# A neighbourhood attention layer rewritten as a preparation stage and an attention stage, with gathered surroundings and scores made twice

## The reference, cut to what matters

```python
x = x + _L0_conv_ref(_gn(x), ...)          # relative positions
x = x + _L1_conv_ref(_gn(x), registers, qkv_w, qkv_b, out_w, out_b)
x = x + _L2_conv_ref(_gn(x), ...)          # relative positions
x = x + _L3_conv_ref(_gn(x), ...)          # rotary, with a mask
# _L1_conv_ref, 12 heads of 16 channels, a window of 7x7 tokens clipped to the image:
qkv = x @ qkv_w.T + qkv_b
reg_kv = registers @ qkv_w[D_MODEL:].T + qkv_b[D_MODEL:]
k_cat, v_cat = concatenate([k, reg_k]), concatenate([v, reg_v])
scores = einsum('bnqe,bnke->bnqk', q, k_cat) / sqrt(16)
scores = where(mask_cat, scores, -1e30)     # 49 neighbours and the 16 registers
o = einsum('bnqk,bnke->bnqe', softmax(scores), v_cat)
return o @ out_w.T + out_b
```

## Time and profile before

| | |
|---|---|
| median of 3 runs | 9050.09 us (9038.95 to 9065.04) |
| the profiled execution | 9057.34 us, of which 9055.6 us are the span of the trace |
| TensorE, VectorE, ScalarE, GpSimd busy | 81%, 58%, 48%, 25% of the span |
| the window layer's two blocks | 2360.21 to 3985.64 us of the span |

### The profile page before, as it was taken

How to read it: one execution, slowest core, us unless ns; L and a number is a source line. 1 busy time by engine, 2 the same in 40 slices (tenths; PEclk the granted TensorE clock), 3 DMA queues, 4 the chain that set the end, 5 groups by cost and what they waited for, 6 DMA issues and landing times. The chain is left out here.

```text
span 9055.6 us, 188790 instructions
## 1 busy us (share of the span) xinstructions
PE 7343.7 (81%) x62744; PEld 4481.5 (49%) x62744; DVE 5241.4 (58%) x8043; ACT 4335.9 (48%) x8449; POOL 2240.3 (25%) x2715
## 2 busy tenths in 40 slices
PE   2999999989388777846998999899556499999998
PEld 2555555555155555534555555555222255555555
DVE  3655555556255555553555555555588666666665
ACT  1444444444265656541444444445111277777776
POOL 2343434343121211214343434332111000000000
PEclk7989999999698999976998999899777799999999
DMA  6757666766433334346767565764312254445443
GB/s 160 134 114 142 124 131 119 138 120 112 110 74 70 74 68 76 69 119 117 142 119 129 115 135 117 132 121 82 101 56 80 78 133 112 122 119 127 116 119 90
DMA packets 536711, 999.82 MB, mean 110 GB/s; under 512 B 102258, under 2 KB 303027, under 8 KB 500211
## 3 DMA queue, kind: packets, MB, share of 16 engines
q1 hardware_dynamic: 479346, 900.50, 45.7%
q0 software_dynamic: 56576, 88.90, 6.5%
HBM read 645.95 MB, written 335.81 MB: 108 GB/s over the span
## 5 line engine op out<-in xcount | busy, mean ns | idle before, releaser
L1676 DVE TENSOR_REDUCE a_nmp<-a_S 128x2 f32<-128x1024 f32 x1536 | 1878.2, 1224 | 1362.7 <-PE a_S L1524 1347.3
L1777 ACT ACTIVATE a_PROB<-a_T 128x512 f32<-128x512 f32 x3072 | 1667.6, 595 | 1959.9 <-PE a_T L1503 1949.0
L1373 POOL CAST a_RF<-a_RL 32x512 fp32r<-32x512 f32 x1536 | 1295.0, 843 | 1120.8 <-DVE a_RL L1704 1028.8
L2492 DVE CUSTOM_DVE_ANT_0 a_X<-a_S,a_mask 128x1024 f32<-128x1024 f32 x768 | 910.0, 1223 | 551.9 <-PE a_S L2388 548.5
L1499 PE MATMUL a_T<-a_QW,a_KW 64*128 64x512 f32 x3072 | 813.4, 522 | 300.4 <-issue 135.3
L2533 ACT ACTIVATE a_PROB<-a_T 128x512 f32<-128x512 f32 x1536 | 835.8, 601 | 382.9 <-PE a_T L2402 382.9
L1499 PEld LDWEIGHTS a_T<-a_QW,a_KW 64*128 64x128 f32 x3072 | 313.8, 193 | 1312.3 <-issue 1309.3
L1537 PE MATMUL a_O<-a_PROB,a_V 128*32 128x512 f32 x6144 | 929.5, 681 | 2.5 <-ACT a_PROB L1777 2.5
L2402 PE MATMUL a_T<-a_ident,a_X 128*128 128x128 f32 x6144 | 824.7, 277 | 101.8 <-DVE a_OSB L2509 98.1
L962 DVE CUSTOM_DVE_ANT_0 a_PROB<-a_S,a_mask 128x512 f32<-128x512 f32 x768 | 522.8, 688 | 591.9 <-PE a_PT L799 498.4
L2402 PEld LDWEIGHTS a_T<-a_ident,a_X 128*128 128x128 f32 x6144 | 671.8, 141 | 303.0 <-issue 285.3
(11 more groups left out here) (158 smaller groups left out, 9847.0 us busy)
## 6 DMA issues: line engine op xcount, KB each, us to landing
a_QV<-a_part_rows SPq DMA_DIRECT2D x384, 256.0 KB, 7.2
a_rel_rows<-a_RF SPq DMA_DIRECT2D x96, 1024.0 KB, 9.2
a_K<-part_rows SPq DMA_DIRECT2D x576, 128.0 KB, 4.0
a_X<-xn_scratch SPq DMA_DIRECT2D x72, 768.0 KB, 6.7
stream<-a_Y POOLq DMA_DIRECT2D x288, 192.0 KB, 4.6
a_part_rows<-a_part SPq DMA_DIRECT2D x48, 1024.0 KB, 12.2
a_QV<-a_part_rows SPq DMA_DIRECT2D x384, 128.0 KB, 7.8
a_QV<-a_rel_rows SPq DMA_DIRECT2D x384, 128.0 KB, 6.4
```

Source lines behind the costliest of these rows:

```text
L1373: nc.gpsimd.tensor_copy(dst, src).then_inc(permuted, 1)
L1676: nc.vector.tensor_reduce(nmp[:, qh, c, 2 * pr:2 * pr + 2, kh], S[:, pr], AX.X, ALU.max).then_inc(s_done, 1)
L1777: nc.scalar.activation(PROB[:, s % PRING, 2 * pr + sd], T[:, slot(("st", s, pr, sd))], ACT.Exp).then_inc(t_act, 1)
L2492: nc.vector.tensor_tensor_reduce(out=X[:, v % 2, c, g], in0=S[:, sd].rearrange("p a b -> p (a b)"), in1=mask[:, n % 2, g, c], scale=1.0, s ...
```

## The change

The window layer's blocks become `prepare_win` and `attend_win`; the other layers keep theirs.

`prepare_win` goes once over the images. It normalises an image, and GpSimd gathers for each quadrant of 16x16 queries the 19x19 tokens around it, with the 16 registers put between their lines: 377 keys, padded to 384. TensorE projects the queries (four pieces of 512), the keys of the four quadrants (eight pieces of 384) and the values (twelve chunks of 128 keys), all heads at once. VectorE and ScalarE split queries and keys in two F32R parts, and SP stores all three in DRAM.

`attend_win` has 24 units again, each now four quadrants ("turns") of 256 queries, and each turn three steps, one for each 128 of its 384 keys. An operand has 79 rows: 48 of split queries or keys, 16 and 13 that code the window's rows and columns (so the mask comes out of the matmul), and 2 that carry the row maximum. The scores are made twice. `straight` makes them queries by keys for the maximum alone, two turns ahead: four items a turn, each two heads, reduced by `row_max`. `combine` splits the maximum, `turn_max` transposes it, and `take_max` writes it into the two rows of the query operand. `transposed` then makes the scores keys by queries, maximum already subtracted; ScalarE exponentiates them from PSUM, and the result is the moving operand of `values` without a transpose or a copy. PSUM tiles for `transposed`, `turn_max` and the tail of the unit before share a ring of three. In a step TensorE issues the first pair of heads of `transposed`, then `values` of the step before, then `straight`, then the second pair.

```diff
-KEYS_W = 4 * P
+NEAR = 3 * P
+NEAR_CHUNKS = 12
...
+def prepare_win(nc, sems, name, x_in, stream_out, w, gavg, q_rows, k_rows, v_rows, near_lines):
+    RING, BLOCKS = 6, 3
+    QUADS = 4
+    ORDER = [("q", m, t) for m in range(2) for t in range(2)]
+    for j in range(6):
+        ORDER += [("k", *divmod(j, QUADS)), ("v", j, 0)]
+    ORDER += [("k", 1, 2), ("k", 1, 3)]
+    PIECES = [n for n in ORDER if n[0] != "v"]
...
+            def gather(b):
+                s = b % 2
+                pool.wait_ge(xn_ready, 2 * b + 2)
+                need(pool, t_ready, done(b - 2, ORDER[-1], "pe") if b > 1 else 0)
+                alone(pool)
+                for quad in range(QUADS):
+                    y, x, n = 13 * (quad // 2), 13 * (quad % 2), before_regs(quad)
+                    image = XN[:, s].rearrange("p k (y x) -> p k y x", x=SIDE)
+                    at = 19 * n
+                    nc.gpsimd.tensor_copy(XG[:, s, :, quad, 0:at].rearrange("p k (y x) -> p k y x", x=19),
+                                          image[:, :, y:y + n, x:x + 19]).then_inc(gathered, 1)
+                    nc.gpsimd.tensor_copy(XG[:, s, :, quad, at + REGS:19 * 19 + REGS].rearrange("p k (y x) -> p k y x", x=19),
...
+                if n[0] == "q":
+                    _, m, t = n
+                    image = XN[:, s].rearrange("p k (y x) -> p k y x", x=SIDE)
+                    for right in range(2):
+                        for k in range(2):
+                            last = nc.tensor.matmul(T[0:HALF, to, 256 * right:256 * right + 256],
+                                                    wq[:, k, m * HALF:(m + 1) * HALF],
+                                                    image[:, k, 16 * t:16 * t + 16, 16 * right:16 * right + 16],
+                                                    start=k == 0, stop=k == 1)
+                elif n[0] == "k":
+                    _, m, quad = n
+                    for k in range(2):
+                        last = nc.tensor.matmul(T[0:HALF, to, 0:NEAR], wk[:, k, m * HALF:(m + 1) * HALF], XG[:, s, k, quad],
+                                                start=k == 0, stop=k == 1)
+                else:
+                    for a in range(2):
+                        quad, c = divmod(2 * n[1] + a, NEAR // P)
+                        here = slice(CHANNELS * a, CHANNELS * a + CHANNELS)
+                        for k in range(2):
+                            nc.tensor.matmul(T[:, to, here], XG[:, s, k, quad, P * c:P * c + P], wv[:, k],
+                                             start=k == 0, stop=False)
+                        last = nc.tensor.matmul(T[:, to, here], one_line[:], bv_line[:], start=False, stop=True)
+                last.then_inc(t_ready, 1)
+
+            pe.wait_ge(consts_loaded, CONSTS)
+            pe.wait_ge(set_up, SETUP)
+            alone(pe)
+            mean(0)
...
+def attend_win(nc, sems, name, stream, w, ident, q_rows, k_rows, v_rows, near_lines):
+
+    UNITS = GROUPS * IMAGES
+    QUADS, CHUNKS_N = 4, NEAR // P
+    STEPS = QUADS * CHUNKS_N
+    RING, PRING, BUFS = 3, 3, 3
+    WIDE = 2 * P
+    ROWS = 3 * DIM + 16 + 2 + 13
+    TURNS_N = QUADS * UNITS
+    SPANS = {(0, 0): (0, 256, 0, 226), (0, 1): (94, 284, 0, 284), (1, 0): (0, 284, 0, 284), (1, 1): (128, 256, 24, 226)}
+    ITEMS = {0: (0, 1), 1: (2,), 2: (3,)}
+    TAIL = {2: "sum", 3: "turn0", 5: "turn1", 6: "wo00", 8: "wo01", 9: "wo10", 11: "wo11"}
+    NM_AT = 1
...
+                for sd in range(2):
+                    g = 2 * pr + sd
+                    last = nc.tensor.matmul(S[:, n % 2, sd, 0:width],
+                                            Q_[0:ROWS, s, g, WIDE * quad + P * tile:WIDE * quad + P * tile + P],
+                                            K[0:ROWS, s, g, NEAR * quad + at:NEAR * quad + at + width], start=True, stop=True)
+                last.then_inc(s_ready, 1)
...
+            def values(u, s):
+                quad, kc = divmod(s, CHUNKS_N)
+                t = QUADS * u + quad
+                pe.wait_ge(t_act, TALLY[("t", u, s, 1)])
+                if s == 0:
+                    pe.wait_ge(v_loaded[u % BUFS], 16 * (u // BUFS + 1))
+                if kc == 0:
+                    need(pe, o_out, t)
+                alone(pe)
+                for g in range(G):
+                    last = nc.tensor.matmul(O[Q * g:Q * g + Q, t % 2], V[:, u % BUFS, s, g], PROB[:, (STEPS * u + s) % PRING, g],
+                                            start=kc == 0, stop=kc == CHUNKS_N - 1)
+                last.then_inc(pv_done, 1)
+
...
+                    transposed(u, s, 0)
+                    if s:
+                        values(u, s - 1)
+                    elif u:
+                        values(u - 1, STEPS - 1)
+                    if t + 2 < TURNS_N:
+                        for i in ITEMS[kc]:
+                            straight(t + 2, i)
+                    transposed(u, s, 1)
+                    if kc == NM_AT and t + 1 < TURNS_N:
+                        turn_max(t + 1)
+                    if u and s in TAIL:
+                        tail(TAIL[s], u - 1)
...
+            def combine(t):
+                e = t % 2
+                eng.wait_ge(s_done, 4 * t + 4)
+                nc.vector.tensor_copy(nm_hi[:, e], nm[:, e]).then_inc(nm_ready, 1)
+                eng.wait_ge(nm_ready, t + 1)
+                nc.vector.tensor_copy(nm_wide[:, e, :, 0:P:Q], plain(nm_hi[:, e])).then_inc(nm_split, 1)
+                nc.vector.tensor_tensor(nm_wide[:, e, :, 1:P:Q], nm[:, e], plain(nm_hi[:, e]), ALU.subtract).then_inc(nm_split, 1)
...
-        normalise_block(nc, sems, f"n{i}", x, xn, streams[i], w["bo"], a["gavg"])
-        if kind == "rel":
...
+            prepare_win(nc, sems, f"n{i}", x, streams[i], w, a["gavg"], q_rows, k_rows, near_rows, near_lines)
+            attend_win(nc, sems, f"a{i}", streams[i], w, a["ident"], q_rows, k_rows, near_rows, near_lines)
...```

On TensorE, two tiles of a unit in `attend_block` before stood so (a_S scores, a_PT the transposed probabilities, a_O outputs):

```order
L799 MATMUL a_PT<-a_ident,a_PROB 128x128 x4
L782 MATMUL a_S<-a_KK,a_QQ 128x384
L782 MATMUL a_S<-a_KK,a_QQ 128x128
L799 MATMUL a_PT<-a_ident,a_PROB 128x128 x4
L814 MATMUL a_O<-a_PTS,a_V 16x128 x16
```

More of the change, by code:

```diff
@@ L317, in attend_block @@
[L317 to L329, removed]
@@ L431, in attend_block @@
-        jobs = []
-        def job(step, pe, dve=(), act=()):
-            jobs.append((step, pe, list(dve), list(act)))
-        def project(w_sb, rows, half):
-            def run(n, par):
-                cols = slice(STARTS[half], STARTS[half] + WIDTHS[half])
-                if rotary:
-                    cols = slice(0, BANK)
-                    if half == 1:
-                        nc.tensor.wait_ge(loaded_more, 16 * 3 * (n + 1))
-                        alone(nc.tensor)
-                for k in range(2):
-                    last = nc.tensor.matmul(M[0:rows, 0:cols.stop - cols.start], w_sb[:, k, :], X[:, k, cols],
-                                            start=k == 0, stop=k == 1)
-                return last
-            return run
@@ L469, in add_v_jobs @@
-        def add_v_jobs(step, halves):
-            for i, half in enumerate(halves):
-                job(step + 2 * i, project(wv_sb, G * DIM, half), act=[v_out(half)])
-                run, place = turn_v(half)
-                job(step + 2 * i + 1, run, act=[place])
-        def free_whole(n, piece):
-            before = UNIT_STEPS * n + SPLIT_STEPS * piece - (REL_STEPS if piece == 0 else 0)
-            need(nc.vector, split, before, solo=True)
-            if rel:
-                need(nc.vector, moved, 16 * G * (PIECES * n + piece), solo=True)
@@ L892, in epilogue, with free @@
-            def epilogue():
-                n = UNITS - 1
-                output(n, 1, CHUNKS - 1)
-                before = lambda: tail_out(pe, n, 0, 2)
-                for half, which in TAIL_AFTER.values():
-                    tail(n, half, which, before)
-                    before = lambda half=half, which=which: tail_out(pe, n, half, which)
-            pairs(pe, prologue, body, epilogue)
+            def free(b, n):
+                i, v = ORDER.index(n) - RING, b
+                if i < 0:
+                    i, v = i + len(ORDER), v - 1
+                if v >= 0:
+                    pe.wait_ge(out_of[kind(ORDER[i])], done(v, ORDER[i], kind(ORDER[i])))
@@ L1018, in _ @@
+            rest(NP * IMAGES - 1)
         @block.scalar
         def _(act):
[L1020 to L1034 removed]
@@ new lines, in values @@
+            def values(b, j):
+                s = b % 2
+                act.wait_ge(t_ready, done(b, ("v", j, 0), "pe"))
+                if j == 0:
+                    need(act, v_stored[s], 16 * (b // 2))
+                alone(act)
+                nc.scalar.copy(VT[:, s, 2 * j:2 * j + 2, :, 0:DIM],
+                               T[:, ORDER.index(("v", j, 0)) % RING, 0:2 * CHANNELS].rearrange(
```

(7 more changed lines are left out.)

1173 lines of the change are left out of this document (536 added, 637 removed).

## The result

| | median us | runs | ratio to before |
|---|---|---|---|
| before | 9044.7 | 10 | |
| changed | 8992.3 (8979 to 9024) | 10 | 0.9944, 95% 0.9930 to 0.9958 |

The account below looks back on a forecast made before the run. The old layer was taken as bound by a ring of four engines' work per tile, none full. The new stages, 319 + 35 + 781 + 29 = 1164 us for 1625.4, gave 8590 us, range 8455 to 8730.

Parts of the forecast that it names:

- The ring: In attend_win, values, straight, second pair and exponential form a loop of 2.22 us a step, 2.58 in a turn's first.
- The pair's pitch of 0.35 us: In attend_win, one transposed pair costs TensorE 0.35 us, between bounds of 0.25 and 0.46 depending on hidden weight loads.
- Cost taken: none; if it did not hide, 3 us an image: In prepare_win, the next image's late load hides behind six PSUM slots of TensorE work; otherwise 3 us an image.
- A slower clock: Rival for attend_win: clock at 0.93 makes the stage 6% longer, 46 us; chance 0.15, shared with a late maximum.
- The start: Before attend_win's first step: constants, code rows and operands take 18 us at 315 GB/s; 35 us in all.
- Weight loads exposed: Rival for attend_win: each pair and item costs 0.46 us instead of 0.35, 84 us more, 8675; chance 0.12.
- cheaper groups: Rival for attend_win: first loads hidden, pitch 0.25 us, 28.5 us a unit, 8495; chance 0.08.
- The rule that I set against the rows: For attend_win: weight loads overlap matmuls only on different row groups, so no 79-row load hides; same 8675 as exposed loads.
- F32R as slow as F32: Rival for attend_win: full-height F32R streams at F32 speed, 615 us more, 9205; chance 0.03.
- DMA bounds prepare_win: Rival for prepare_win: at 180 GB/s an image takes 44 us, 72 more in all, 8660; chance 0.03.
- Late maximum: Rival for attend_win: take_max ends 0.3 us late behind turn_max, 29 us; chance 0.15, shared with a slower clock.
- no change: Rival for the whole change: all the gain lost in waits, 20 us a unit; chance 0.01.

Follow-up runs that it names:

- e9_best: Changed kernel with output copies early, loads an image ahead, operands loaded buffer by buffer, and three added 480-column matmuls among the sums: 8569 us, ratio 0.9449.
- e1: Changed kernel with the output copy made between the exponentials of a turn's first step instead of its second: 8734 us, ratio 0.9655.
- e3: Changed kernel with each image's load in the prepare stage issued one image earlier, ahead of the stores: 8872 us, ratio 0.9800.
- e12: Changed kernel with output copies early and an unused 512-column matmul added ahead of each item of scores: 8959 us, ratio 0.9874.
- e2: Changed kernel with an unused 512-column matmul added ahead of each item of scores, output copies still late: 9034 us, ratio 0.9979.
- e6: Changed kernel with output copies early, loads an image ahead, and three unused 480-column matmuls among each unit's sums: 8609 us, ratio 0.9498.
- e7: Changed kernel with output copies early, loads an image ahead, and code rows and operands loaded together buffer by buffer: 8619 us, ratio 0.9520.
- e11: The kernel of e7 with each unit's 16 short sum rows issued as two groups of 8, three steps apart: 8614 us, ratio 0.9498.

## Why the prediction was wrong

The layer's terms in us, forecast, changed kernel, and the kernel with its faults mended:

| | forecast | changed | e9_best |
|---|---|---|---|
| prepare_win | 319 | 436.7 | 315.4 |
| start of attend_win | 35 | 63.4 | 38.4 |
| 24 units (one) | 781 (32.5) | 1097.3 (45.7) | 789.0 (32.9) |
| end | 29 | 23.9 | 25.2 |
| layer | 1164 | 1621.2 | 1168.0 |

The sum describes e9 to 4 us, but that is partly luck. The ring was right. The pair's pitch of 0.35 us was too high (0.24, below), and e9 does 2.4 us a unit of added work that the forecast doesn't have. The best units of e1, without that work and with the clock low for less than 4 us, took 31.6 us from sums to sums, where 32.5 stood. The rate at the start of `attend_win` was wrong by more than half. What the sum took for granted is a TensorE at its upper clock level whose waits I had all listed. Both assumptions failed.

- **"Cost taken: none; if it did not hide, 3 us an image"**, said of the next image's load, failed, in its place and in its price. The load did land late ("perhaps 14 us into the image", 16.7 us after its issue in the image shown), but I counted TensorE's six slots as cover and not what is queued behind the wait on VectorE, which empties those slots. It cost 31.9 us in seven images itself, and some 55 to 90 through the clock (e3, against the profiles with the old stage).
- **The ring of attend_win** (exponential to `values`) is there as worked out: at the upper level a step with `turn_max` takes 2.11 us in e9 where 2.22 stood (below, from one `values` to the next). What failed is the sentence before it, that `values` waits for the exponential: in a turn's first products it also waits for `outputs`, through `need(pe, o_out, t)`, and ScalarE's order put that copy behind another exponential. 4.4 us a unit at the upper level, 105 us (shown by e12 against e2). It could be read in the code.

TensorE's timeline in e9:

```profile
3043.38 0.64 PE L813 MATMUL a_O<-a_PROB,a_V 128*32 128x256 f32 x8
3043.95 0.52 PE L784 MATMUL a_S<-a_K,a_Q 79*128 79x284 f32 x2
3044.31 0.40 PE L798 MATMUL a_T<-a_Q,a_K 79*128 79x256 f32 x2
3044.55 0.38 PE L823 MATMUL a_T<-a_ident,a_nm_wide 128*128 128x128 f32 x2
3044.69 0.48 PE L798 MATMUL a_T<-a_Q,a_K 79*128 79x256 f32 x2
3045.49 0.64 PE L813 MATMUL a_O<-a_PROB,a_V 128*32 128x256 f32 x8 [0.32 <-ACT a_PROB L957]
```

- **"A slower clock ... at 0.93 the stage would take 6% more, 46 us"** named the right mechanism and took its size from the wrong stage. I set the clock by the 0.93 of `attend_block`; it was 0.63, and the 1.00 of `attend_rot` is a mix with other work. Of the 316 us that the units took beyond the forecast, about 105 were the wait and the rest, about 210, the clock. That is a subtraction, and since the forecast unit was some 1 us too long, the clock's part may be 20 us more. For 145 of them e1 shows it; e6 wins back another 42 although its columns cost 2.4 us a unit. With the clock at 1.00 e9's units are within 0.1 us of the 32.5 forecast; the stage's last 8 us over it come mostly from its first 49 us at the lower level.
- **The start**: 18 constant DMAs and operands were priced at 315 GB/s, as the 21 us window of `prepare_rot` moved them; the stretch ran at 132, and 28 us were missed. With the order changed the rate stayed at 141 (e7). Why these loads are so slow wasn't tried.
- **Rivals.** *Weight loads exposed* is out: in the rows above the second pair has a pitch of 0.24 us (3044.31 to 3044.55), the bound of *cheaper groups* and not the 0.35 that I took, and the item 0.36, as costed, not 0.46. The rule that I set against the rows, the Trainium skill's ("TensorE: Matmul & The Clock Gate", Part 3, The mechanism), by which no load of a 79-row operand would hide, is not borne out (the same section also lets a load for a background weight buffer go ahead, and no run here tells whether it is that): two matmuls of 256 columns alone take 0.21 at the pitch of the earlier trace rows, which leaves no room for an exposed load of 0.107. *F32R as slow as F32* is out by the same 0.24. *DMA bounds prepare_win* is out by e3's 315.5 us. *Late maximum*: 6.7 us of waits in the changed kernel and 26 in e9, where I had 29.
- **Chances.** Faster came true, but by luck, as far as the two profiles show: the time came from a neighbour, and within the layer the change was worth 4 us, and "no change", which I gave 0.01 because it "would need all of the gain lost in waits, 20 us a unit", is what the layer did. 13 us a unit were lost, and 118 in the prepare stage, which I hadn't put in that case.

## What to carry to other kernels

For every wait of TensorE in a new stage ask what it does to the clock, not only how long it lasts: here 147 us of waits (115 and 31.9), taken away, gave back 340 to 370 with the clock that they had taken along, so a stage that is forecast full to the brim at the upper level needs a second sum at the lower one. List the waits of a step from the code, semaphore by semaphore with what stands ahead of each increment on its engine, and for a wait on VectorE or ScalarE list what is queued behind it. When a stage is slower than its sum, look at the granted clock first: a copy moved one step up and a load moved one image up, a few lines each, were worth 258 and 120 us.

## What the runs showed of the hardware

- TensorE without a gap stayed long at the lower clock level: 24 us of keys and values in a row at 0.50 (changed kernel, 2418 to 2442), and 34 us of a unit with two gaps of 1.1 to 1.2 us (3048 to 3082). In the changed kernel's units 25 of 27 rises had a projection of 512 columns in the 5 us before them, but only 17 of 23 in e1 and 8 of 23 in e11: such a product isn't needed for a rise.
- It fell after waits of 1.1 to 1.4 us in a stretch of 256-column products, and after 1.8 us (or 0.95) of rows of 4 columns with waits of 0.2 to 0.5 us before them; with long products between (e2) it fell after one of 95 such waits, stayed down for less than 4 us each time, and was at 0.98 on the mean. Which property of the work decides isn't settled here.
- VectorE's RECIPROCAL took 3.36 us for 512 columns of 128 rows from PSUM, where a multiplication took 0.69.
- The same code in an unchanged `attend_rel` layer took 2332 to 2398 us in fourteen profiles, at a mean clock of 0.92 in the shortest and 0.87 in the longest.
